# Who writes the normed rows and the softplus inputs: four per-token multiply-adds and two step inputs moved from VectorE to ScalarE

## The reference

```
def _layernorm(x, axis=-1, eps=1e-05):
    m = jnp.mean(x, axis=axis, keepdims=True)
    v = jnp.var(x, axis=axis, keepdims=True)
    return (x - m) / jnp.sqrt(v + eps)
...
    h = _layernorm(x, axis=-1) * (1 + ca) + sa
    x = x + ga * _L0_attn_ref(h, ...)
    h = _layernorm(x, axis=-1) * (1 + cb) + sb
    x = x + gb * _L0_ffn_ref(h, ...)
...
            delta = jax.nn.softplus(jnp.einsum('bld,ed->ble', delta_in, dt_proj_w) + dt_proj_b)
            A = -jnp.exp(A_log)
            def step(h, inp):
                dt, bt, ct, xt = inp
                dA = jnp.exp(dt[:, :, None] * A[None])
                h = dA * h + dt[:, :, None] * bt[:, None, :] * xt[:, :, None]
                y = jnp.einsum('bds,bs->bd', h, ct) + D * xt
                return (h, y)
```

## Time and profile before

| what | value |
|---|---|
| time, median of 3 runs | 3391.09 us (3389.65 to 3392.9) |
| the profiled execution's own time | 3393.52 us |
| its span, first to last instruction | 3392.3 us |
| DVE, ACT busy | 2613.5 us, 1557.9 us |
| POOL busy | 1210.9 us |

### The profile page before, as it was taken

One profiled execution on the slowest core, in us unless ns is written; L12 is line 12 of the kernel. 1 busy time (PEld: TensorE's weight loads), 2 busy tenths in 40 slices (PEclk: granted clock), 3 DMA queues, 4 the chain that ended last, 5 costly groups with the idle time before them and its releaser, 6 DMA issues. The chain is left out here.

```text
span 3392.3 us, 34666 instructions
## 1 busy us (share of the span) xinstructions
PE 2336.6 (69%) x8947; PEld 1154.7 (34%) x8947; DVE 2613.5 (77%) x6691; ACT 1557.9 (46%) x3364; POOL 1210.9 (36%) x1118
## 2 busy tenths in 40 slices
PE   3068775876648786797758786487866876586854
PEld 1015222542215431363215531154313632164313
DVE  4874899779987799858898699977899588964282
ACT  2406722675226752467226652167524682263322
POOL 3020336314343153513454143341545143631471
PEclk8579787978869897797979887698878989697857
DMA  3011012131011311131110410113101311102212
GB/s 92 0 28 26 25 45 58 40 95 47 33 49 32 102 53 32 50 93 55 45 52 25 122 52 24 49 34 103 57 29 49 103 50 42 52 18 89 66 38 87
DMA packets 118905, 181.35 MB, mean 53 GB/s; under 512 B 15824, under 2 KB 55392, under 8 KB 115552
## 3 DMA queue, kind: packets, MB, share of 16 engines
q1 hardware_dynamic: 114528, 170.05, 17.9%
q0 software_dynamic: 4096, 8.40, 0.9%
HBM read 156.51 MB, written 21.89 MB: 53 GB/s over the span
## 5 line engine op out<-in xcount | busy, mean ns | idle before, releaser
L1324 POOL TENSOR_TENSOR gat<-sil,cbs 128x512 f32<-128x512 f32 x256 | 324.1, 1268 | 372.7 <-ACT sil L1289 272.1
L736 DVE TENSOR_SCALAR_CACHE_REDUCE wmask<-z,tc 128x512 bf16<-128x512 f16 x640 | 436.0, 741 | 23.4 <-ACT z L703 19.2
L1520 ACT ACTIVATE ps_rest<-cols,Aneg 128x512 f32<-128x512 f32 x256 | 175.8, 689 | 417.8 <-DVE hfc L1540 384.5
L904 POOL TENSOR_SCALAR wmask<-wmask 128x512 bf16<-128x512 bf16 x256 | 163.0, 637 | 482.4 <-DVE wmask L861 477.4
L1264 PE MATMUL ps_rest<-rest_hT,WF 128*128 128x512 f32 x512 | 291.2, 656 | 29.0 <-ACT sil L1289 28.8
L987 PE MATMUL ps_att<-z,Vp 128*32 128x128 f32 x2048 | 282.6, 285 | 20.2 <-DVE z L1059 20.2
L1254 PE MATMUL ps_rest<-gat,WP 128*128 128x512 f32 x512 | 280.0, 631 | 4.6 <-POOL gat L1324 4.3
L1289 ACT ACTIVATE sil<-ps_rest,w_b1T 128x512 f32<-128x512 f32 x256 | 174.1, 685 | 213.9 <-PE ps_rest L1264 209.0
L1037 DVE CUSTOM_DVE_ANT_0 z<-ps_att,wmask 128x512 f32<-128x512 f32 x256 | 175.6, 686 | 119.3 <-PE ps_att L975 111.9
L669 PE MATMUL ps_att<-qk 128*128 128x512 bf16 x512 | 221.7, 448 | 66.4 <-DVE g_rank L852 25.8
L1492 PE MATMUL ps_rest<-hg,ident 128*128 128x512 f32 x256 | 197.6, 864 | 98.9 <-DVE hg L1552 98.6
(11 more groups left out here) (358 smaller groups left out, 5280.2 us busy)
## 6 DMA issues: line engine op xcount, KB each, us to landing
cbs<-spreads SPq DMA_DIRECT2D x128, 256.0 KB, 3.4
WF<-in_w SPq DMA_DIRECT2D x64, 256.0 KB, 2.6
WP<-in_w SPq DMA_DIRECT2D x64, 256.0 KB, 2.6
WF<-in_wfc SPq DMA_DIRECT2D x64, 256.0 KB, 2.6
WG<-in_wgate SPq DMA_DIRECT2D x64, 256.0 KB, 2.9
WP<-in_wproj SPq DMA_DIRECT2D x64, 256.0 KB, 3.3
qk<-bounce SPq DMA_DIRECT2D x32, 384.0 KB, 6.0
bounce<-both_parts SPq DMA_DIRECT2D x72, 128.0 KB
```

Source lines behind the costliest of these rows:

```text
L736: od.up(dve.tensor_scalar(wmask[:, i, :], z_at[i], tc[:, 0, i:i + 1], None, ALU.is_ge, ALU.add, accum_out=tc[:, 1, i:i + 1]))
L1324: weighed0.up(pool.tensor_tensor(gat[m % 2], sil[m % 2], cbs[e % 2][:], ALU.mult))
L1520: decays.up(act.activation(dA[k][:], dl[:, k, :], ACT.Exp, scale=Aneg[:, k, s:s + 1]))
```

## The change

`act_norm` gets the source tiles and writes the four normed tiles itself, before it waits for the transposes: an activation of kind Identity with two columns, scale `rstd` and bias `less`. `less` is minus the mean times `rstd`, which DVE now forms for all four tiles in one instruction of four elements per row and signals as `centred`. DVE's four tensor_scalar instructions are gone. In the softplus, ACT writes v (Identity with bias) and |v| (Abs with bias) straight from each bank, four instructions per batch, and releases `soft` with each; DVE's three instructions are gone. The yields, the lengths that the planner uses, change with them: 0.30 for each of ACT's four, 0.22 for `less`, 0.73 for each softplus input.

```diff
+            self.less, self.centred = sb(name + "_less", [P, NT]), sig(name + "_centred", norms)
...
-    soft, softe, logged, stepped, y_open, zeroed = sig("soft"), sig("softe"), sig("logged"), sig("stepped"), sig("y_open"), sig("zeroed")
+    soft, softe, logged, stepped, zeroed = sig("soft", 2 * DC), sig("softe"), sig("logged"), sig("stepped"), sig("zeroed")
...
-    def act_norm(w, b, k, bank, scale, shift, dst):
+    def act_norm(w, b, k, bank, scale, shift, dst, src):
+        yield w.centred.at(b, k)
+        act.wait_ge(*w.centred.at(b, k))
+        for j in range(NT):
+            w.normal.up(act.activation(w.nrm[:, j, :], src[:, j, :], ACT.Identity, bias=w.less[:, j:j + 1], scale=w.rstd[:, j:j + 1]))
+            yield 0.30
         yield w.turned.at(b, k)
...
         dve.wait_ge(*w.rooted.at(b, k))
-        for j in range(NT):
-            w.normal.up(dve.tensor_scalar(w.nrm[:, j, :], src[:, j, :], w.mv[:, j, 0:1], w.rstd[:, j:j + 1],
-                                          ALU.subtract, ALU.mult))
-            yield 0.36
+        w.centred.up(dve.scalar_tensor_tensor(w.less[:], w.mv[:, :, 0], -1.0, w.rstd[:], ALU.mult, ALU.mult))
+        yield 0.22
...
-        yield soft.at(b)
-        act.wait_ge(*soft.at(b))
         e = dtx.rearrange("p k t -> p (k t)")
+        for m in range(DC):
+            yield dt_ps.at(b, m)
+            act.wait_ge(*dt_ps.at(b, m))
+            soft.up(act.activation(yz[m], bk[m][:], ACT.Identity, bias=wts["dt_b"][:, m:m + 1]))
+            yield 0.73
+            soft.up(act.activation(dtx[:, m, :], bk[m][:], ACT.Abs, bias=wts["dt_b"][:, m:m + 1]))
+            yield 0.73
+        yield soft.all(b)
+        act.wait_ge(*soft.all(b))
         softe.up(act.activation(e, e, ACT.Exp, scale=-1.0))
...
-        for m in range(DC):
-            yield dt_ps.at(b, m)
-            dve.wait_ge(*dt_ps.at(b, m))
-            od.up(dve.tensor_scalar(yz[m], bk[m][:], wts["dt_b"][:, m:m + 1], None, ALU.add))
-            yield 0.78
         v, e, q = (t.rearrange("p k t -> p (k t)") for t in (hg2[:], dtx, hfc2[:]))
-        od.settle()
-        soft.up(dve.scalar_tensor_tensor(e, v, -1.0, v, ALU.mult, ALU.max))
-        yield 1.27
```

More of the change, by code:

```diff
@@ L274, in emit @@
     proj_in, split_in, conved, xed = sig("proj_in", 4), sig("split_in", 4), sig("conved", 2), sig("xed", 2)
-    din_ps, dins, dt_ps, dts = sig("din_ps", 2), sig("dins", 2), sig("dt_ps", 2), sig("dts")
-    soft, softe, logged, stepped, y_open, zeroed = sig("soft"), sig("softe"), sig("logged"), sig("stepped"), sig("y_open"), sig("zeroed")
+    din_ps, dins, dt_ps = sig("din_ps", 2), sig("dins", 2), sig("dt_ps", 2)
+    soft, softe, logged, stepped, zeroed = sig("soft", 2 * DC), sig("softe"), sig("logged"), sig("stepped"), sig("zeroed")
     keptB, outB, spreadB, spreadC = sig("keptB"), sig("outB", 1, 16), [sig(f"spreadB{i}", NS // 4, 16) for i in range(4)], sig("spreadC", NS)
@@ L564, in act_prepare @@
         bk, mod = prepare_banks(b), modT[0][:, b]
-        yield from act_norm(att, b, 0, bk[0], mod[:, 1:2], mod[:, 0:1], att.hT)
+        yield from act_norm(att, b, 0, bk[0], mod[:, 1:2], mod[:, 0:1], att.hT, xr[b % 3])
         yield k_ps.at(b)
@@ L1181, in act_mixture0 @@
         mod = modT[0][:, b]
-        yield from act_norm(rest, b, 0, rest.bank[0], mod[:, 4:5], mod[:, 3:4], c1)
-        yield from act_norm(rest, b, 1, rest.bank[0], wts["g1"][:], wts["be1"][:], c0)
-        yield from act_norm(rest, b, 2, rest.bank[0], wts["g2"][:], wts["be2"][:], rest.hT)
+        yield from act_norm(rest, b, 0, rest.bank[0], mod[:, 4:5], mod[:, 3:4], c1, xr[b % 3])
+        yield from act_norm(rest, b, 1, rest.bank[0], wts["g1"][:], wts["be1"][:], c0, in_tiles(rest.bank[1]))
+        yield from act_norm(rest, b, 2, rest.bank[0], wts["g2"][:], wts["be2"][:], rest.hT, in_tiles(rest.bank[1]))
         yield expl.at(b, 0)
@@ L1368, in act_mamba @@
         c = ((rest.c[0], rest.c[1]), (rest.c[2], cbs[0]))
-        yield from act_norm(rest, b, 3, rest.bank[0], modT[1][:, b, 1:2], modT[1][:, b, 0:1], rest.hT)
+        yield from act_norm(rest, b, 3, rest.bank[0], modT[1][:, b, 1:2], modT[1][:, b, 0:1], rest.hT, xr[b % 3])
         for k in range(2 * DC):
@@ L1625, in act_mixture1 @@
         mod = modT[1][:, b]
-        yield from act_norm(rest, b, 4, rest.bank[0], mod[:, 4:5], mod[:, 3:4], rest.hT)
+        yield from act_norm(rest, b, 4, rest.bank[0], mod[:, 4:5], mod[:, 3:4], rest.hT, xr[b % 3])
         yield expl.at(b, 1)
```

## The result

The changed kernel takes 3416.01 us (3409.26 to 3423.5), the kernel before beside it 3392.76 (3389.65 to 3396.01): a ratio of 1.0069, 95% interval 1.0056 to 1.0082. The profiled execution took 3417.0, its span 3415.7, 23.4 more than before. 3376 was predicted; the sign was wrong. The time lies near the slower rival's 3411.

A forecast was written before the change was run, and what follows sets the result against it. DVE was busiest (82%), but ACT was full as the first mixture starts, DVE in the long middle, PE in the last regime. Per batch -0.4 - 2.6 + 0.5 = -2.5, times 7, ends +2.3: -15 us, 3376; range 3345 to 3402.

The forecast's parts named there:

- the slower rival: ACT becomes the bound at the refill, its list waiting there for the shift: total +20 us, 3411; chance 0.23.
- the first mixture: Stage with three rest norms, refill copies and search: together -0.4 us per crowded batch, from -1.2 to +3.7.
- norm one: First mixture, source `xr`: +0.5 us latency; its 1.44 on ACT lengthens the refill, remainder taken at nothing.
- Norm three: First mixture, on DVE between two search rounds: DVE loses 1.36 us and gains 0.17, so -1.2.
- Norm two: First mixture, source PSUM: +0.3 us latency; ACT's 1.44 nearly covered by its 1.71 us wait for PE.
- the routed mixture: Last stage, PE full, so DVE's relief is worth nothing: +0.5 us per batch, from 0 to +1.0.
- the ends: Batch 0's attention norm +0.5, batch 7's norms +2.1, its softplus -0.2: together +2.3 us or so.
- the state space block: Own norm 0, attention norm -1.2, softplus -1.8: together -3.0 us per batch, 0.9 of it taken, -2.6.
- the softplus: State space block: DVE -2.7 us, 0.9 given back on average waiting for the Exp; -1.8 remains, bounds -2.7 and -1.2.
- ACT's waits for `rest_less`: Sign against the forecast: wrong if ACT's refill copies show waits for `rest_less`; no size given.
- DVE's wait for signs: Sign against the forecast: wrong if DVE's wait for ACT's signs grows beyond its 38.5 us by more than 15.
- DVE's -65 to -75 and ACT's 90: Whole-kernel busy times: DVE's should fall by 65 to 75 us, to about 2543; ACT's rise by about 90.

The follow-up runs named there:

- e6: Only norm two of the first mixture written by ACT, all else as in the kernel before: 3439.35 us, ratio 1.0032 to that kernel.
- e5: Only norm one of the first mixture written by ACT, all else as in the kernel before: 3434.66 us, ratio 1.002 to that kernel.
- the second pair: Traces of the kernel before and the changed kernel, both timed again without edits: ratios 0.9999 and 1.0071 to the kernel before.
- e13: The changed kernel timed again without edits: 3413.9 us, 1.007 of the kernel before; its trace is of its longest run, 3423.98.
- e3: Only the softplus' value and magnitude on ACT, all six norms as in the kernel before: 3381.38 us, ratio 0.9979 to that kernel.
- e1: The changed kernel with the first mixture's three norms back on DVE: 3387.26 us, ratio 0.999 to the kernel before.
- e2: Only the first mixture's three norms on ACT, all else as in the kernel before: 3415.34 us, ratio 1.0076 to that kernel.
- e4: The changed kernel with the softplus back on DVE, all six norms on ACT: 3418.05 us, ratio 1.0083 to the kernel before.

## Why the prediction was wrong

**The step that failed** is the first mixture, put at -0.4 us a batch and measured at +3.0. Its parts: norm one was given +0.5 for its way, with "I take the remainder at nothing" for ACT's 1.44. Measured +1.8 up to its copy in batches 1 to 6. I had looked for cover of ACT's time (the 1.71 us idle) and not asked what DVE's time had been covered by: ACT's copies of the routed results, of which the earlier trace rows shows two at 1919.16. (That is batch 4, the one where DVE began its four only behind them; in the other six DVE's four overlap them.) Norm three was given -1.2 because DVE's 1.36 fell away between two rounds; measured +1.5 up to its copy. In batch 4 the time that it sets free on DVE goes into the wait for ACT's signs (1.23 us in the row above), and in all six its way through ACT, with signs before it or behind it, lies on the chain, which I had counted for norms one and two only. Norm two's price (5.2 in e6) is hidden, not by ACT's idle time but, as e5's 4.9 suggests, by what DVE did ahead during norm one.

In us, the forecast's -15 and the measured +23.4 are 38 apart, in round numbers: 24 are the first mixture, 8 the routed mixture, 8 the ends, and the state space block is 1 better.

**The rival** had place and sign right: ACT at the refill. Its +4.1 above the forecast a batch was near (+3.4). Its mechanism holds for the shift that waits in ACT's list, but not for its price: the 1.24 of waiting for POOL was no new loss, and the copies of the routed results, which it did not name, were.

A rule of the Trainium skill spoke against the move (ScalarE: Activation LUTs, Rules for kernel authors: additions and multiplications belong to VectorE). Per tile the trace agrees, 486 and 453 ns against the 348 and 403 of the earlier trace rows. But the price of a tile did not decide alone: the routed results' copies and the signs did more, norms of the same price elsewhere cost 6 us in all, and the softplus inputs, moved against the same rule, gained 8.

**State space block and experts**: -2.6 forecast, -2.6 measured (-2.5 in the second pair). With e13's trace it is -1.4 or -0.9, so that the number fits so well is in part luck. Of it the softplus alone gives -1.4 (e3), against a forecast of 1.8 x 0.9 = 1.6. In batch 7 the Exp starts 2.61 us behind PE's end (2.64 forecast), at once behind the table load:

```profile
3234.41 3.60 PE L1362 MATMUL ps_rest<-hfc,w_dt_projT 128*128 128x512 f32 x8
...
3239.32 1.28 ACT L1413 ACT_TABLE_LOAD   x1
3240.62 1.06 ACT L1413 ACTIVATE cols<-cols 128x1024 f32<-128x1024 f32 x1
3241.69 1.28 ACT L1417 ACT_TABLE_LOAD   x1
...
3242.99 1.06 ACT L1417 ACTIVATE cols<-cols 128x1024 f32<-128x1024 f32 x1
```

The load now lies open, as counted, and nothing is added to it: the load ends at 3240.60, the Exp begins at 3240.62. The drain of about 1.38 us that the Trainium skill adds to a switch (same page, What ACT_TABLE_LOAD costs) is not there, as in the earlier trace rows. DVE waits for the Exp in six batches, not in half of them, but for little:

```profile
DVE hfc L1446 <- ACT cols L1413: 6.8, 6, 3.6
```

**Routed mixture**: +0.5 forecast, +1.9 measured (+1.2 with e13's trace). e3 has +0.7 in that stage, e1 +1.7, e2 +1.0, e4 +2.1. So the norms seem to bring more of it than the softplus, wherever they stand, though traces of one kernel lie up to 0.7 apart. PE is busy in it for 352.6 us instead of 344.2, at a clock mostly 0.95 instead of 0.97. What makes it so I have not shown.

**Ends**: 2.3 forecast, 10.1 measured. Batch 0 has 8.7 of it, 4.8 before its first Exp; I had counted only one norm there.

**Sum**: 13.3 in the four stages of the table and 10.1 around them. Of the signs named as proof against me, ACT's waits for `rest_less` came true, though only 29.5 of the 118.8 us are there in e2, which has them in the first mixture alone; DVE's wait for signs grew by 13, less than the 15 I had set; the refill's end is 3 us later. DVE's -65 to -75 and ACT's 90 were right, and told nothing of the time.

## What to carry over

Before moving work from the busiest engine to a less busy one, look at the chain that the result is on: what ran beside the old instruction on the engine that takes it over? That was the cover, and it turns into a queue. An engine's share over the whole span (49%) hides the 20 us in which its list is full; a serial stage takes the relief of one engine as a wait for the other. And time a small gain in more than one set of runs: one kernel here stood at 0.994 in one and at 1.003 in another.

## What I had not expected of the chip

Two-column activations of 128 columns take 479 ns from SBUF and 455 from PSUM (medians), and four in a row 1.65 and 1.50 us: each further one adds 0.39 and 0.35, where two copies of 512 columns from PSUM had saved 0.12. The same kernel's time moved by 40 us of 3390 between sets of runs at nearly one granted clock (0.80 to 0.82 in either kind of set), with PE waiting for weights in most traces of the longer ones.
